# Stacked queries and keys transposed in three DMAs each, and the second stack of batch 0's pass prepared in another order

## Time and profile before

| what | value |
|---|---|
| median of 3 runs | 429.08 us (427.14 to 429.15) |
| the profiled execution, its own time | 429.13 us |
| its span, first to last instruction | 427.3 us |
| mean granted TensorE clock, share of full | 0.996 |
| TensorE busy, over the span | 394.0 us (92%) |
| ScalarE | 371.0 us (87%) |
| VectorE | 348.8 us (82%) |
| GpSimd | 288.5 us (68%) |

### The profile page before, as it was taken

One profiled execution on the slowest core, in us unless ns is written; L12 is line 12 of the kernel. 1 busy time (PEld: TensorE's weight loads), 2 busy tenths in 40 slices (PEclk: granted clock), 3 DMA queues, 4 the chain that ended last, 5 costly groups with the idle time before them and its releaser, 6 DMA issues.

```text
span 427.3 us, 13356 instructions
## 1 busy us (share of the span) xinstructions
PE 394.0 (92%) x5403; PEld 221.6 (52%) x5403; DVE 348.8 (82%) x903; ACT 371.0 (87%) x497; POOL 288.5 (68%) x365
## 2 busy tenths in 40 slices
PE   0689999898999799999999999999999999999995
PEld 0346666674454445535545546446454336676655
DVE  5889999689799978988988988957769938888565
ACT  4799999776898689899898998999988989999961
POOL 5679999986624956767768658662223558999951
PEclk9999999999999999999999999999999999999999
DMA  6487523513714417418347047046123115556452
GB/s 172 102 195 156 69 49 51 100 27 74 126 28 100 75 20 95 88 30 109 66 65 120 17 77 125 3 92 110 38 42 75 27 36 80 109 122 108 117 123 81
DMA packets 119298, 35.25 MB, mean 82 GB/s; under 512 B 101697, under 2 KB 119233, under 8 KB 119233
## 3 DMA queue, kind: packets, MB, share of 16 engines
q1 hardware_dynamic: 117952, 34.02, 43.3%
q10 hardware_dynamic: 1280, 0.33, 0.3%
HBM read 4.98 MB, written 4.19 MB: 21 GB/s over the span
## 4 chain that ended last, share of the span: by engine, by line
PE 59%; DVE 9%; ACT 9%; DMA 7%; POOL 7%; issue 5%; SPq 1%; ACTq 0%; DVEq 0%
PE ps L754 11%; PE ps L519 11%; PE ps L784 11%; PE ps L791 10%; PE ps L583 4%; PE ps L572 4%; DMA QKT<-ST 4%; PE ps L818 4%; ACT XN L471 3%; PE ps L608 3%; ACT PT L898 2%; PE ps L761 2%; DVE H L340 2%; POOL HL L446 2%; ACT SG L489 2%
## 5 line engine op out<-in xcount | busy, mean ns | idle before, releaser
L898 ACT ACTIVATE PT<-ps,k_exp 128x1024 f32<-128x1024 f32 x144 | 153.6, 1117 | 14.4 <-PE ps L761 7.9
L519 PE MATMUL ps<-XT,WT 128*128 128x512 f16 x384 | 94.0, 383 | 5.8 <-DVE H L340 1.9
L754 PE MATMUL ps<-QKT 128*32 128x512 f16 (+1 forms) x1280 | 86.7, 361 | 5.6 <-DMA QKT<-ST 4.5
L791 PE MATMUL ps<-PT,ones 128*32 128x512 f32 (+3 forms) x768 | 76.7, 488 | 0.0
L784 PE MATMUL ps<-PT,V 128*32 128x512 f32 (+3 forms) x768 | 76.3, 487 | 0.0
L446 POOL TENSOR_TENSOR HL<-H,HH 128x1024 f16<-128x1024 f32 x31 | 66.5, 2145 | 8.4 <-ACT HH L495 5.4
L340 DVE SCALAR_TENSOR_TENSOR H<-SG,k_isilu,ps 128x1536 f32<-128x1536 f32 x31 | 56.1, 1809 | 11.2 <-ACT SG L489 5.8
L519 PEld LDWEIGHTS ps<-XT,WT 128*128 128x128 f16 x384 | 34.4, 98 | 50.3 <-issue 10.1
L471 ACT ACTIVATE XN<-X,NB,RS 128x128 f32<-128x128 f32 x128 | 52.5, 483 | 2.4 <-POOL NB L418 2.4
L754 PEld LDWEIGHTS ps<-QKT 128*32 128x32 f16 x1280 | 31.9, 97 | 41.3 <-issue 22.6
L489 ACT ACTIVATE SG<-ps,k_silu 128x1536 f32<-128x1536 f32 x32 | 48.8, 1525 | 4.4 <-DVE H L340 4.3
(11 more groups left out here) (146 smaller groups left out, 671.2 us busy)
## 6 DMA issues: line engine op xcount, KB each, us to landing
result<-X SPq DMA_DIRECT2D x15, 256.0 KB, 2.5
X<-in_L_attn_x SPq DMA_DIRECT2D x7, 512.0 KB, 4.6
X<-in_L_attn_x SPq DMA_DIRECT2D x2, 256.0 KB, 4.7
XT<-w_int SPq DMA_TRANSPOSE x32, 3.1
QKT<-ST SPq DMA_TRANSPOSE x20, 5.5
AXT<-AS SPq DMA_TRANSPOSE x16, 2.8
w_int<-in_L_ffn_w_gate SPq DMA_DIRECT2D x1, 192.0 KB, 3.9
w_int<-in_L_ffn_w_up SPq DMA_DIRECT2D x1, 192.0 KB, 4.4
```

Source lines behind the costliest of these rows:

```text
L519: i = e.matmul(out[:, j, :], WT[:, wp, w * NJ + j, :], XT[k % 2][:, xp, :], start=a == 0, stop=a == len(passes) - 1)
L754: i_ = e.matmul(dst[r, :].rearrange("p (s a n) -> p s a n", a=2, n=P), QKT[k % 2][:, i // TPC, NH + hp, key0 + r.start:key0 + r.stop], q.r ...
L791: i_ = e.matmul(sums_of(h, 1, n), ones32[:, :], weights_of(g, h, o, n), start=i == 0, stop=i >= TPC * qc, skip_group_check=True)
L898: e.activation(dst, SCORES[(SLOT0[g] + i) % 2][:, :, :], ACT.Exp, scale=k_exp[:, 0:1]).then_inc(a_exp, 1)
```

## The change

On TensorE, `scores` now waits piece by piece in every batch: at group 0 for the keys and first queries, then (hp = 1) for the second queries; at group 3 for the two query pieces of the second chunk, at group 7 for its keys. On SP, `qk` issues every stack in three DMAs: keys, first and second queries for even m; first queries, second queries, keys for odd m. For m = 3 the transpose of x's chunk 5 stands ahead of the keys.

In step k = 0 only: vector does the second chunk's (m = 3) sums, norms and unit before it normalises chunk 5, and `stack_hi2` of chunk 3 right behind that, ahead of the stats of chunks 6 and 7 and add_norm of chunk 4. ScalarE casts chunk 3 at g = 8 rather than 9 and splits x's chunk 5 at g = 9 rather than 7. GpSimd takes x's low part of chunk 5 behind the stack's low parts.

The branch `shift` is for large temperatures and isn't taken with these inputs.

```diff
@@ scores (TensorE)
-                if g == 0 and isinstance(b, int) and b == 0 and not shift:
+                if shift:
+                    if hp == 0 and tiles_[0][0] == 0:
+                        e.wait_ge(d_u[qc], b * 16 + 16)
+                elif g == 0:
                     if hp == 0:
-                        e.wait_ge(d_k0, 16)
-                        e.wait_ge(d_q0, 16)
+                        e.wait_ge(d_k0, b * 16 + 16)
+                        e.wait_ge(d_q0, b * 16 + 16)
                     else:
-                        e.wait_ge(d_t[0], 16)
-                elif g == G0 and isinstance(b, int) and b == 0 and not shift:
-                    e.wait_ge(d_q2 if hp else d_q1, 16)
-                elif g == NG - 3 and isinstance(b, int) and b == 0 and not shift:
-                    e.wait_ge(d_t[1], 16)
-                elif hp == 0 and tiles_[0][0] == 0:
-                    e.wait_ge((d_u if shift else d_t)[qc], b * 16 + 16)
+                        e.wait_ge(d_t[0], b * 16 + 16)
+                elif g == G0:
+                    e.wait_ge(d_q2 if hp else d_q1, b * 16 + 16)
+                elif g == NG - 3 and hp == 0:
+                    e.wait_ge(d_t[1], b * 16 + 16)
@@ step of ScalarE
-                        if g == (9 if k == 0 else 8):
+                        if g == 8:
                             stack_hi(m0 + 1, 1)
                     if k + 2 < B and g == 7:
                         x_hi(m0 + 2, 0)
+                    if k + 2 < B and g == (9 if k == 0 else 7):
                         x_hi(m0 + 3, 1)
@@ step of GpSimd
                 if later:
                     x_lo(m0 + 2, 0)
+                if later and k >= 1:
                     x_lo(m0 + 3, 1)
                 if nxt:
                     stack_lo(m0 + 1, 1)
+                if k == 0:
+                    x_lo(m0 + 3, 1)
@@ step of VectorE
-                if later:
+                if later and k >= 1:
                     normalise(m0 + 3, m0 + 3, q + 1)
...
                     unit(k + 1, 20 * b + 40, m0 + 1, 1)
+                if k == 0:
+                    normalise(m0 + 3, m0 + 3, q + 1)
                 if nxt:
                     rows(m0, k, b, 0)
+                if k == 0:
+                    stack_hi2(m0 + 1, 1)
                 if k + 3 < B:
                     stats(m0 + 4, m0 + 4, 2 - q)
                     if k == 0:
                         stats(m0 + 5, m0 + 5, 3 - q)
                         add_norm(e, m0 + 2, m0 + 2, q)
-                if nxt:
+                if nxt and k >= 1:
                     stack_hi2(m0 + 1, 1)
@@ qk(m) and its calls (SyncE)
-                if m == 0 and not shift:
-                    stack(0, NH, NQK, d_k0)
-                    stack(0, 0, 2, d_q0)
-                    stack(0, 2, NH, d_t[0])
-                    return
-                if m == 1 and not shift:
-                    stack(1, 0, 2, d_q1)
-                    stack(1, 2, NH, d_q2)
-                    stack(1, NH, NQK, d_t[1])
-                    return
-                stack(m, 0, NQK, d_t[m % 2])
                 if shift:
+                    stack(m, 0, NQK, d_t[m % 2])
                     e.wait_ge(a_mx, 3 * m + 3)
                     stack(m, 0, NH, d_u[m % 2])
+                elif m % 2:
+                    stack(m, 0, 2, d_q1)
+                    stack(m, 2, NH, d_q2)
+                    if m == 3:
+                        turn_x(e, 5)
+                    stack(m, NH, NQK, d_t[1])
+                else:
+                    stack(m, NH, NQK, d_k0)
+                    stack(m, 0, 2, d_q0)
+                    stack(m, 2, NH, d_t[0])
 
             for k in range(B):
                 qk(2 * k)
                 if k == 0:
                     qk(1)
-                for half in range(2):
-                    if k + 1 < B:
-                        turn_x(e, 2 * k + 2 + half)
-                if k:
+                if k + 1 < B:
+                    turn_x(e, 2 * k + 2)
+                if k + 1 < B and (k != 1 or shift):
+                    turn_x(e, 2 * k + 3)
+                if k >= 1:
                     qk(2 * k + 1)
```

## The result

| what | before | changed |
|---|---|---|
| median of 6 runs each | 428.91 us (427.14 to 429.99) | 424.99 us (424.72 to 425.62) |
| ratio, 95% interval | | 0.9919 (0.9901 to 0.9936) |
| profiled execution, its own time | 429.13 us | 424.84 us |
| its span | 427.3 us | 423.0 us |

What follows compares the result with a forecast made beforehand. TensorE bounds a steady batch; 5.6 us hang on late transposed stacks and the clock behind them. Gains of 2.5 (batch 1), 0.72 (chunk 5) and 0.1 (later) make 3.3: 429.1 to 425.8 us, range 423.4 to 428.8.

Steps and rivals of the forecast that it cites:

- QN of chunk 3: Vector, batch 0's pass: four normalise instructions (1.07 us) leave from ahead of the sums, so QN is done at 132.7.
- Stack 3's issue: SP: issues the first piece of stack 3 at about 135.8, 3.5 us sooner.
- The copies: Vector's two second copies of chunk 3 are held by GpSimd's two instructions until about 135.8; wo_out(0) ends some 0.35 later.
- What is late next: Batch 1: ScalarE waits for ON, done at 145.1, so weighing g3 comes at 149.05 instead of 151.55, 2.5 us gained.
- Chunk 5's x: Its AXT transpose lands at 141.1 to 143.5, asked for by TensorE at 143.3; costs nothing, at worst 0.2 us.
- Chunk 5 and later: Pieces remove TensorE's 0.72 us wait at chunk 5 and an estimated 0.1 us in later batches.
- New waits: Rival: later exps(1, g0) or a clock dip take 1.0 to 2.7 us of the gain; say 427.5 us, chance 0.17.
- The full gain: Rival: ON comes 1.5 us sooner or more, nothing replaces the stall, 5.6 us gained; 423.5 us, chance 0.12.
- Little changes: Rival: GpSimd's and vector's copies block each other, so stack 3 leaves SP no sooner; 428.6 us, chance 0.12.
- Pieces that don't overlap: Rival: DMA pieces land in series, 9.6 us for three, costing 0.8 us in each of six batches; 430.6 us, chance 0.08.
- (1): Batch 0's reordering on vector, ScalarE and GpSimd: stack 3 is ready sooner, its first piece issued 3.5 us sooner.
- (2): Stacks in three pieces on SP: first piece lands in 4.6 us, third in 6.5; chunk 3's queries land at 140.4 and 141.7.

Runs made afterwards that it cites:

- ON later: Changed kernel plus an unused 256-column reciprocal on vector ahead of o_norm(1) in batch 1; median 426.84 us, ratio 0.9972 to the kernel before.
- both waits moved: Changed kernel with add_norm of chunk 5 behind chunk 4's unit and chunk 5's x transposed between stack 3's query pieces; 424.62 us, ratio 0.9911 to the kernel before.
- order alone: Kernel before with only the reordering on vector, ScalarE and GpSimd, whole stacks, chunk 5's x behind stack 3; 425.16 us, ratio 0.9930.

## Why the prediction was right

*QN of chunk 3.* Forecast 132.7, came at 132.75 (131.79 + 0.96), with the two stretched steps where they were counted: 1.15 us at 127.97 behind OL's split, 1.07 at 130.68 behind chunk 4's low part.

*Stack 3's issue.* Forecast 135.8, came at 135.65, 3.67 us sooner.

*The copies.* Here a term was mis-sized. I let GpSimd hold both second copies until 135.8. The first slipped in at 133.69, against GpSimd's start at 133.70, and the second took 1.19 us, to 135.08: it was held by the first of GpSimd's two instructions (until 134.99) and not by the second. So vector's work behind them ran 0.8 us sooner: wo_out(0) no longer delayed the second projection (I had booked 0.35 us), ON ended at 144.37 instead of 145.1, exps(g3) began at 145.42 instead of 146.3, and g3 came at 148.16 instead of 149.05. From exps to weighing it was 2.74 us, forecast 2.75. So g3 gained 3.4 us where 2.5 were forecast. The Trainium skill (SBUF — State Buffer, Who interferes with whom) says that whoever issues first gets the pair, and the trace agrees: the copy that started 0.01 us ahead ran in 0.29 us, as it does alone, and the one that came behind was held.

*What is late next.* As forecast, ScalarE waits for ON (1.65 us until 144.41), the chain runs through it, TensorE's waits ahead of group 4 are short and the clock stays up. *ON later* moved g3 by as much as it moved ON (1.56 and 1.55 us).

*Chunk 5's x.* Forecast to land by 143.5 and cost 0.2 us at worst. It landed at 143.2 (138.37 + 4.8) and TensorE, being early, waited 0.66. This cost nothing: V's copy stood behind OH until 144.94 anyway.

*Chunk 5 and later.* 0.82 us forecast, 1.07 in the two traces (4.44 us of gain at batch 4's first scores less 3.37 at batch 2's), 1.4 in the medians of one job. The reason held only in part: it is not that a whole stack always lands too late there, but that it lands near enough to its time to be late in some executions. Neither chunk 4 nor a steady batch shows a wait for a piece.

*The sum.* 3.3 us forecast, 4.3 between the profiled executions (429.13 to 424.84) and 3.9 between the medians: the profiled execution of before lies 0.2 us above its median, that of the changed kernel 0.15 below. So the mechanism was right and the size was low: each of its two main terms measured more than it was booked at.

*The rivals.* New waits and a dip of the clock did not come. The full gain did not come either; half of the 2.1 us by which batch 1 still exceeds a steady one was reached by *both waits moved* (30.8), and half of that was given back in batch 2 (30.2). Little changes: the cast came 2.9 us sooner, the copies were done 4.2 us sooner, and SP issued 3.7 us sooner. Pieces that don't overlap: those of a stack were issued 1.3 to 2.6 us apart (3.1 where chunk 5's x stood between), and the slowest of 48 landed in 5.9 us, the median in 4.0. The Trainium skill (DMA: Bandwidth & Descriptors, Rules for kernel authors) would have many small transfers joined, and names 64 KB as the size below which one pays mostly overhead; a piece has 0.26 MB, four times that. The prediction's estimate from its figures, 2.6 us for a piece, was low: none of the 48 landed in less than 3.1. Here, where the first third of a stack is asked for long before the last and the queue moves the pieces one close behind another, splitting gained 1.4 us in the later batches.

What the prediction did not say is that either of its two halves is nearly enough by itself: it built batch 1's gain on (1) and (2) together, and either alone gives 3.0 to 3.4 us, against 3.5 for both by the ratios.

## What to carry to other kernels

When a wait is removed, look along the same engine queues for what would have been ready only a little before it: here ON stood 1.7 us ahead of the late stack, and capped two independent remedies at nearly the same gain. A stall of TensorE of some microseconds is priced with the clock behind it; unused matmuls in it are a quick test of that part, and by themselves gave 1.5 us. Before an instruction is moved back on one engine, look for who waits for it on the others: a 1.1 us add_norm moved off one path held GpSimd for 4.5 us, and half of the gain or more was lost in the next batch.

## What was not expected of the hardware

Chunk 5's whole stack, behind two AXT transposes, took 8.6 us to land in the kernel before and 6.4 in *order alone*; TensorE waited 0.72 us for it in the one, not at all in the other, and 0.54 in a third kernel. With the later stacks split the kernel was steadier as well as faster: 5 runs within 0.24 us, against 10 within 2.1 us on the same chip. Of 54 runs of the kernel before 14 had a mean clock of 0.999 or 1.0, where 40 had 0.996 or less. And in *ON later*, with 1.41 us as TensorE's longest wait in the trace, 4 of 10 runs had a clock as low as the kernel before had with a wait of 2.80.
